# A graph layer and a mixture-of-experts block on one core: rows of x on more transfer engines, edge counts in two groups, four bank pairs in the first layer

## The chip, the cores and the metric

The kernel runs on one core of a Trainium2 chip. The time is device microseconds (us) of one execution. The engines are called as in the profile: PE is TensorE (PEld its weight loads), DVE is VectorE, ACT is ScalarE, POOL is GpSimd, SP is SyncE; SPq and ACTq are their queues of issues.

## The reference

x has 625 rows of 1024 float32; src and dst are 10000 edges, dst sorted.

```python
def layernorm(x): return (x - mean(x)) / sqrt(var(x) + 1e-05)
# graph layer, on xn = layernorm(x), edges (src, dst) and one self edge per row
h = xn @ W.T + b
deg = count of edges (with self) by row = src
out[row] += deg[row]**-0.5 * deg[col]**-0.5 * h[col]
x = x + out
# block, on t = layernorm(x)
h = t @ lin0_w + lin0_b
h = silu(h @ swi1_w1 + swi1_b1) * (h @ swi1_w2 + swi1_b2)
scores = softmax(h @ gate_w.T)                    # 8 experts, the best 4, renormalised
routed = sum over the 4 of weight * (silu(h @ w1) * (h @ w3)) @ w2
shared = (silu(h @ sh_w1) * (h @ sh_w3)) @ sh_w2
h = (routed + shared) @ lin1_w + lin1_b
x = x + silu(h @ swi2_w1 + swi2_b1) * (h @ swi2_w2 + swi2_b2)
```

## The kernel before

**Tiles and units.** The 625 rows are five tiles of TT = 125 rows, in `rows`. Dense layers work on transposed activations [128 features, 8 chunks, 628 tokens] (625 and three of padding, two halves of HT = 314). A *unit* is 128 output features of a layer: one 512 KB block of the weight stream. It comes by SP into one of four `raw` slots. ACT copies it into a rounded high part (`split_hi`, L384) and POOL subtracts that for the low part (`split_lo`, L392). PE multiplies high by high, high by low and low by high (`products`, L1323): 48 matmuls for a unit over two banks, one bank for each half. `half_unit` does one half. A reader on ACT and one on DVE then take the result out of the banks as a high and a low part again. Each engine runs a list written out by hand; semaphores order the engines.

**The start.** SP issues the two index arrays, five transfers for the tiles of x (L344), then the weights. For each tile ACT sums the rows (L530) and the squares (L525). After the last one DVE makes the variance (L834), ACT takes the root (L536), splits the first weight unit and waits for the shift (L839). ACT then normalises tile by tile (L541), PE turns each tile by 8 transposes (`xt_turn`, L1314), ACT and DVE copy the high and the low part (`xt_high` L548, `xt_low` L812).

**Counting edges.** The layer needs the matrix of edge counts, 625 by 625. The edges lie as 80 *slots* of 125. For a slot DVE builds a one-hot of dst (L769) and one of src folded into 314 columns (L770), in which an edge of the upper half weighs 4096 and one of the lower half 1. PE adds 5 matmuls for it into five banks (L1298); `OHR = 4` slots are a *batch* (PE) or *iteration* (DVE), and DVE may be four slots ahead. The slots come in three groups of 32, 32 and 16 (`GROUPS`). A group is opened by 5 matmuls with zeros (L1292) and closed by 5 more (L1304). DVE then decodes each of the five banks into a lower and an upper count (`decode`, L789 to L801); the next group may open when the banks are read (`banks_read`). The first decoding also adds the identity.

**Units of the graph layer.** PE's order is batches 0 to 6, turns 0 and 1, batch 7, closing, turns 2 and 3, the first half of unit 0, turn 4, the second half, unit 1, batches 8 to 11, unit 2, batches 12 to 15, closing, units 3 and 4, the third group (batches 16 to 19), units 5 and 6, the degrees (25 matmuls of one column, L1438), unit 7. Within unit m, PE turns the output of unit m-1 back into rows (`h_turn_first`, L1379) and the last tile of unit m-2 (`h_turn_last`, L1386); these need DVE's low parts `h_low` (L819) and `h_low_last` (L825) of the unit before. ACT and DVE scale the counts by the root of the degrees (L580, L882). Then come ten aggregations and the second normalising (`root`, `ln_high`, `ln_low`, `ln_turn`).

**The first layer, lin0.** Units 0 and 1 are done in halves in banks 0 to 3; units 2 to 7 use banks 0, 1 and 2, 3 in turn, each after DVE's low part of the unit two before (L1520). Ahead of that ACT issues the save of the rows (x1, 2.5 MB, L624) and the load of the gate's weights (L625).

## Time and profile before

| what | us |
|---|---|
| median of 3 runs | 1656.29 |
| lowest and highest | 1655.44, 1656.95 |
| the profiled execution, its own time | 1656.63 |
| its span from first to last instruction | 1655.0 |
| PE busy in the span | 1606.2 |
| DVE, ACT and POOL busy | 491.9, 520.2 and 783.8 |

The time is that of the whole execution; the span runs from the first to the last instruction in the trace. The trace gives start times from the start of the span. A row of a timeline has the start, the time from the first start to the last end of the merged instructions, the engine and line, the operation with its output and inputs, the count, and in brackets the idle time before it with what ended it. A matmul's time holds its way through the array, so pace is read from starts. The granted clock in a window is a share of 2.4 GHz.

### The profile page before, as it was taken

Reading aid. Unit: us, or ns where it says so; the run is one execution under the profiler, and the core shown is the slowest. Engines: PE = TensorE matmul, PEld = TensorE weight load, DVE = VectorE, ACT = ScalarE, POOL = GpSimd, SP = SyncE. Lnnn points to the kernel's source line nnn. Section 1 sums busy time; section 2 is a strip of 40 time slices with the busy share of each in tenths; the row PEclk is TensorE's granted clock in tenths of the full one; section 3 lists DMA queues with packets and bytes.
Section 4 is the critical chain, followed back from the end, with each engine's and each line's share of the span. In section 5 each row is a group of like instructions: output and inputs, shape, how many; then the busy total and the mean of one; then the engine's idle time right before and its main releaser. Section 6 shows DMA issues by size and latency. Waiting matters only on the chain.

```text
span 1655.0 us, 28056 instructions
## 1 busy us (share of the span) xinstructions
PE 1606.2 (97%) x11047; PEld 1588.0 (96%) x11047; DVE 491.9 (30%) x898; ACT 520.2 (31%) x745; POOL 783.8 (47%) x396
## 2 busy tenths in 40 slices
PE   6889989999999999999999999999999899999997
PEld 5789889999999999999999999999999899999997
DVE  5865621111541011414132242424221044111011
ACT  4312123222222234334444434444444222222120
POOL 1211023332352465766767586767677566333330
PEclk8999999999999999999999999999999999999999
DMA  4301032223232254645555464646465566233220
GB/s 128 125 27 39 1 126 77 77 68 126 73 99 77 87 152 130 205 141 183 155 176 170 147 202 140 209 141 209 152 185 156 154 180 181 77 104 111 71 74 34
DMA packets 64355, 205.62 MB, mean 124 GB/s; under 512 B 13228, under 2 KB 14478, under 8 KB 64248
## 3 DMA queue, kind: packets, MB, share of 16 engines
q1 hardware_dynamic: 44718, 157.88, 32.1%
q0 software_dynamic: 14976, 32.81, 6.4%
q10 hardware_dynamic: 4554, 13.32, 2.2%
q8 instruction: 89, 1.46, 0.4%
q14 instruction: 18, 0.15, 0.0%
HBM read 185.01 MB, written 18.95 MB: 123 GB/s over the span
## 4 chain that ended last, share of the span: by engine, by line
PE 91%; DVE 3%; issue 2%; DMA 1%; POOL 1%; ACT 1%; SPq 0%; POOLq 0%; DVEq 0%; ACTq 0%
PE acc L1323 84%; PE acc L1298 2%; DMA rows<-x_dram 1%; PE acc L1603 1%; PE acc L1582 1%; POOL gath L436 1%; POOL w_lo L392 1%; PE acc L1370 0%; DVE yrow L769 0%; DVE gath L801 0%; PE acc L1438 0%; DVE gath L795 0%; DVE gath L793 0%; PE acc L1651 0%; PE acc L1468 0%
## 5 line engine op out<-in xcount | busy, mean ns | idle before, releaser
L392 POOL TENSOR_TENSOR w_lo<-raw,w_hi 128x1024 fp32r<-128x1024 f32 x296 | 713.6, 2419 | 761.6 <-ACT w_hi L384 756.0
L1323 PE MATMUL acc<-act_b,w_hi 128*128 128x314 f32 (+8 forms) x2560 | 518.6, 311 | 0.0
L1323 PE MATMUL acc<-act_x,w_hi 128*128 128x344 f32 (+7 forms) x2048 | 451.7, 309 | 2.3 <-POOL w_lo L392 1.7
L1323 PEld LDWEIGHTS acc<-act_b,w_hi 128*128 128x128 f32 x2560 | 409.9, 189 | 0.0
L1323 PE MATMUL acc<-act_a,w_hi 128*128 128x314 f32 x1792 | 353.3, 314 | 11.3 <-issue 5.4
L1323 PEld LDWEIGHTS acc<-act_x,w_hi 128*128 128x128 f32 x2048 | 342.3, 188 | 3.9 <-issue 3.2
L1323 PE MATMUL acc<-act_b,w_lo 128*128 128x314 f32 (+8 forms) x1280 | 332.1, 308 | 0.0
L384 ACT ACTIVATE w_hi<-raw 128x1024 fp32r<-128x1024 f32 x296 | 310.7, 1050 | 46.2 <-PE acc L1323 34.8
L1323 PE MATMUL acc<-act_x,w_lo 128*128 128x344 f32 (+7 forms) x1024 | 316.3, 309 | 0.0
L1323 PEld LDWEIGHTS acc<-act_a,w_hi 128*128 128x128 f32 x1792 | 288.6, 193 | 12.2 <-issue 5.6
L1323 PEld LDWEIGHTS acc<-act_b,w_lo 128*128 128x128 f32 x1280 | 225.1, 189 | 0.0
L1323 PE MATMUL acc<-act_a,w_lo 128*128 128x314 f32 x896 | 218.7, 311 | 0.0
L1323 PEld LDWEIGHTS acc<-act_x,w_lo 128*128 128x128 f32 x1024 | 192.6, 188 | 0.0
L1323 PEld LDWEIGHTS acc<-act_a,w_lo 128*128 128x128 f32 x896 | 156.2, 192 | 0.0
L1134 DVE TENSOR_TENSOR prod<-acc,silu 128x344 f32<-128x344 f32 x64 | 33.0, 515 | 290.9 <-PE acc L1323 278.3
L1137 DVE TENSOR_TENSOR act_b<-prod,act_b 128x344 fp32r<-128x344 f32 x64 | 99.8, 1559 | 35.7 <-ACT act_b L684 34.6
L684 ACT ACTIVATE act_b<-prod 128x344 fp32r<-128x344 f32 x64 | 31.5, 492 | 187.4 <-DVE prod L1134 173.4
L1126 DVE COPY yrow<-acc 128x256 f32<-128x256 f32 x64 | 27.1, 423 | 165.6 <-PE acc L1603 165.4
L1298 PE MATMUL acc<-yrow 125*125 125x314 bf16 x400 | 62.2, 321 | 13.2 <-DVE yrow L770 13.2
L1298 PEld LDWEIGHTS acc<-yrow 125*125 125x125 bf16 x400 | 58.2, 149 | 17.1 <-DVE yrow L770 15.2
L961 DVE SCALAR_TENSOR_TENSOR prod<-acc,bias,silu 128x628 f32<-128x628 f32 x16 | 13.9, 872 | 192.9 <-PE acc L1323 192.9
L690 ACT ACTIVATE prod<-acc 128x344 f32<-128x344 f32 x64 | 29.3, 457 | 133.4 <-PE acc L1323 133.4
(189 smaller groups left out, 884.1 us busy)
## 6 DMA issues: line engine op xcount, KB each, us to landing
raw<-stream_dram SPq DMA_DIRECT2D x296, 512.0 KB, 3.7
y_dram<-yrow POOLq DMA_DIRECT2D x16, 512.0 KB
rows<-x_dram ACTq DMA_DIRECT2D x2, 2500.0 KB
y_dram<-yrow POOLq DMA_DIRECT2D x8, 352.0 KB
rows<-x_dram SPq DMA_DIRECT2D x5, 500.0 KB
x_dram<-rows ACTq DMA_DIRECT2D x1, 2500.0 KB
h_rows_dram<-rows ACTq DMA_DIRECT2D x1, 2500.0 KB
out_dram<-rows ACTq DMA_DIRECT2D x1, 1250.0 KB
```

The lines of the kernel that those rows point to most:

```text
L384: nc.scalar.activation(w_hi[:, s, :], raw[:, s, :], ACT.Copy).then_inc(hi_split, 1)
L392: nc.gpsimd.tensor_tensor(w_lo[:, s, :], raw[:, s, :], w_hi[:, s, :].bitcast(f32), ALU.subtract).then_inc(lo_split, 1)
L436: pool.indirect_dma_start(out=grow[0:cn, n, :], out_offset=None, in_=h_rows_dram, in_offset=bass.IndirectOffsetOnAxis(ap=now_tok[0:cn, n:n ...
L684: act.activation(g_hi[:, m, :], prod[:, m % 2, 0:CAP], ACT.Copy).then_inc(exp.hi, 1)
L690: act.activation(prod[:, m % 2, 0:CAP], acc[:, m % 4, 0:CAP], ACT.Copy).then_inc(yt_copied, 1)
L1126: dve.tensor_copy(yrow[:, 0:2, m * P:(m + 1) * P], b[:, 0:2 * P].rearrange("p (s d) -> p s d", d=P))
L1134: dve.tensor_tensor(prod[:, m % 2, 0:CAP], acc[:, (2 * m + 1) % 4, 0:CAP], silu[:, 0:CAP], ALU.mult).then_inc(exp.prod, 1)
L1137: dve.tensor_tensor(g_lo[:, m, :], prod[:, m % 2, 0:CAP], g_hi[:, m, :].bitcast(f32), ALU.subtract).then_inc(exp.lo, 1)
L1298: last = pe.matmul(outs[i], oh_dst[0:TT, s, i * TT:(i + 1) * TT], oh_src[0:TT, s, :], start=False, stop=False)
L1323: ins = pe.matmul(o, w, xs_[h], start=(first and w is hi and xs_ is x_hi), stop=(last and w is lo))
L1582: last = pe.transpose(acc[:, TPB + 2 + m % 2, c0:c0 + cn], grow[0:cn, n, m * P:(m + 1) * P], ident[0:cn, 0:cn])
L1603: last = pe.transpose(acc[0:cn, TPB + m % 2, n * P:(n + 1) * P], prod[:, m % 2, c0:c0 + cn], ident[:, :])
```

## The change

The tiles of x come in two transfers each, of 112 and of 13 rows; SP issues tiles 0, 2 and 4, ACT tiles 1 and 3. ACT takes a root of a constant first, and splits the first weight unit ahead of the root of the variance. There are two groups of 40 slots. A group opens with 5 matmuls of one partition that write a negative offset, its last batch carries the closing flag, and the decoding uses 5120 and the offset in place of 4096. Batches and turns alternate from turn 0 on, the low part of h 0 stands before the decoding of the last tile, and the degrees stand before unit 5. ACT saves x1 tile by tile behind each root, and loads the gate's weights before the first root into another buffer. Lin0 uses four pairs of banks.

```diff
@@ -15,7 +15,9 @@
-GROUPS = (32, 32, 16)
+GROUPS = (40, 40)
+BASE = 5120
+BIAS = 2048
@@ -132,7 +134,7 @@
-        gate_raw = gath[:, 0:D]
+        gate_raw = yrow[:, 0, :]
@@ -141,6 +143,7 @@
+        ones16 = scratch16[:, 5416:5416 + 126]
@@ -158,7 +161,7 @@
-        zeros = pw[:, 800:800 + HT // 2].bitcast(bf16)
+        below = pw[:, 800:800 + HT // 2].bitcast(bf16)
...
@@ -336,12 +338,18 @@
+        SPREAD = TT // 16 * 16
+
+        def load_x(eng, i):
+            for r0, r1 in ((0, SPREAD), (SPREAD, TT)):
+                eng.dma_start(rows[r0:r1, i, :], x[i * TT + r0:i * TT + r1, :]).then_inc(x_loaded[i], 16)
+
...
-            for i in range(NT):
-                sp.dma_start(rows[0:TT, i, :], x[i * TT:(i + 1) * TT, :]).then_inc(x_loaded[i], 16)
+            for i in range(0, NT, 2):
+                load_x(sp, i)
@@ -399,7 +407,8 @@
-            pool.memset(zeros[:, :], 0.0).then_inc(const_ready, 1)
+            pool.memset(below[:, :], -float(BASE * BIAS)).then_inc(const_ready, 1)
+            pool.memset(ones16[:, :], 1.0).then_inc(const_ready, 1)
@@ -413,7 +422,7 @@
-            pool.wait_ge(counts_done, len(GROUPS))
+            pool.wait_ge(onehot_used, EC)
@@ -520,21 +529,26 @@
+            for i in range(1, NT, 2):
+                load_x(act, i)
+            act.wait_ge(const_ready, 5)
+            act.activation(rstd[0:TT, 0:1], ones[0:TT, 0:1], ACT.Sqrt)
+
...
-                act.wait_ge(x_loaded[i], 16)
+                act.wait_ge(x_loaded[i], 32)
...
+            split_hi(0, 0)
...
-            split_hi(0, 0)
@@ -572,7 +586,7 @@
-                if m == KC - 1:
+                if m == 5:
@@ -610,26 +624,32 @@
+            def save_x1(i):
+                act.dma_start(x1_dram[i * TT:(i + 1) * TT, :], rows[0:TT, i, :]).then_inc(x1_saved, 16)
+
+            act.dma_start(gate_raw, gate).then_inc(gate_loaded, 16)
...
+            save_x1(0)
...
+            save_x1(1)
...
+            save_x1(2)
...
+            save_x1(3)
...
-            act.wait_ge(gnn_x1, len(AGG))
-            act.dma_start(x1_dram.rearrange("(i p) d -> p i d", p=TT), rows[0:TT, :, :]).then_inc(x1_saved, 16)
-            act.dma_start(gate_raw, gate).then_inc(gate_loaded, 16)
+            save_x1(4)
...
-            def linear_hi(st, o_hi, b):
+            def linear_hi(st, o_hi, b, pairs):
...
-                    act.activation(halves(o_hi[:, m, :]), acc_dense(m % 2), ACT.Identity,
+                    act.activation(halves(o_hi[:, m, :]), acc_dense(m % pairs), ACT.Identity,
@@ -646,7 +666,7 @@
-            linear_hi(lin0, b_hi, B_LIN0)
+            linear_hi(lin0, b_hi, B_LIN0, 4)
@@ -733,7 +753,7 @@
-            linear_hi(lin1, b_hi, B_LIN1)
+            linear_hi(lin1, b_hi, B_LIN1, 2)
@@ -745,7 +765,7 @@
-            act.wait_ge(x1_saved, 16)
+            act.wait_ge(x1_saved, 16 * NT)
@@ -762,16 +782,16 @@
-            link(dve.tensor_scalar(src_v[0:TT, :], src_v[0:TT, :], 4095.0, 1.0, ALU.mult, ALU.add))
-            dve.wait_ge(const_ready, 6 + EXPERTS)
+            link(dve.tensor_scalar(src_v[0:TT, :], src_v[0:TT, :], float(BASE - 1), 1.0, ALU.mult, ALU.add))
+            dve.wait_ge(const_ready, 7 + EXPERTS)
...
-                dve.tensor_scalar(oh_dst[0:TT, s, 0:T], iota[0:TT, 0:T], dst_f[0:TT, j], None, ALU.is_equal)
+                dve.tensor_scalar(oh_dst[0:TT, s, :], iota[0:TT, 0:T + 1], dst_f[0:TT, j], None, ALU.is_equal)
...
-            def iteration(it):
-                for s in range(OHR):
+            def iteration(it, part=range(OHR)):
+                for s in part:
@@ -782,19 +802,19 @@
-                    dve.wait_ge(counts_done, g + 1)
+                    dve.wait_ge(onehot_used, sum(GROUPS[:g + 1]))
...
-                link(dve.tensor_scalar(upper, v, 1.0 / 4096, -0.5 + 2.0 ** -13, ALU.mult, ALU.add))
+                link(dve.tensor_scalar(upper, v, 1.0 / BASE, -0.5 + 2.0 ** -6, ALU.mult, ALU.add))
...
-                    dve.scalar_tensor_tensor(out=low, in0=upper, scalar=-4096.0, in1=v,
+                    dve.scalar_tensor_tensor(out=low, in0=upper, scalar=-float(BASE), in1=v,
...
-                    link(dve.tensor_copy(high, upper))
+                    link(dve.tensor_scalar(high, upper, float(BIAS * len(GROUPS)), None, ALU.add))
...
-                    dve.scalar_tensor_tensor(out=lower_c[0:TT, :], in0=upper, scalar=-4096.0,
+                    dve.scalar_tensor_tensor(out=lower_c[0:TT, :], in0=upper, scalar=-float(BASE),
@@ -833,25 +853,30 @@
-            iteration(5)
+            iteration(5, range(0, 2))
...
+            iteration(5, range(2, OHR))
...
-            for i in range(1, NT):
-                xt_low(i)
-            for i in range(NT):
+            xt_low(1)
+            iteration(8)
+            xt_low(2)
+            iteration(9)
+            xt_low(3)
+            xt_low(4)
+            for i in range(4):
...
-            iteration(8)
...
-            for it in range(9, 13):
+            decode(0, 4)
+            for it in range(10, 16):
...
-            for it in range(13, 16):
+            for it in range(16, 20):
@@ -860,31 +885,28 @@
-            iteration(16)
...
-            for it in range(17, 20):
-                iteration(it)
-            decode(2, 0)
-            decode(2, 1)
-            h_low_last(3)
-            decode(2, 2)
-            h_low(4)
-            decode(2, 3)
-            decode(2, 4)
-            h_low_last(4)
-            h_low(5)
...
-            for i in range(NT):
+
+            def counts_low(i):
...
-                if i == 1:
-                    h_low_last(5)
-            h_low(6)
+
+            counts_low(0)
+            counts_low(1)
+            h_low_last(3)
+            counts_low(2)
+            counts_low(3)
+            counts_low(4)
+            for m in range(4, 7):
+                h_low(m)
+                if m < 6:
+                    h_low_last(m)
@@ -942,10 +964,10 @@
-            def linear_lo(st, o_hi, o_lo, b):
+            def linear_lo(st, o_hi, o_lo, b, pairs):
...
-                    dve.scalar_tensor_tensor(out=halves(o_lo[:, m, :]), in0=acc_dense(m % 2),
+                    dve.scalar_tensor_tensor(out=halves(o_lo[:, m, :]), in0=acc_dense(m % pairs),
@@ -966,14 +988,14 @@
-            linear_lo(lin0, b_hi, b_lo, B_LIN0)
+            linear_lo(lin0, b_hi, b_lo, B_LIN0, 4)
...
-                    dve.wait_ge(x1_saved, 16)
+                    dve.wait_ge(x1_saved, 16 * NT)
...
@@ -1281,7 +1303,7 @@
-            pe.wait_ge(const_ready, 6 + EXPERTS)
+            pe.wait_ge(const_ready, 7 + EXPERTS)
@@ -1289,20 +1311,16 @@
-                    pe.matmul(outs[i], zeros[0:TT, 0:TT], zeros[0:TT, 0:HT], start=True, stop=False)
-
-            def batch(it):
+                    pe.matmul(outs[i], ones16[0:1, 0:TT], below[0:1, 0:HT], start=True, stop=False)
+
+            def batch(it, closes=False):
...
+                    ends = closes and s == OHR - 1
...
-                                         oh_src[0:TT, s, :], start=False, stop=False)
+                                         oh_src[0:TT, s, :], start=False, stop=ends)
...
-
-            def close_counts():
-                for i in range(NT):
-                    last = pe.matmul(outs[i], zeros[0:TT, 0:TT], zeros[0:TT, 0:HT], start=False, stop=True)
-                last.then_inc(counts_done, 1)
@@ -1401,36 +1419,31 @@
                 half_unit(U_GNN, m, a_hi, a_lo, GNN_BANKS[1], 1, turn_first).then_inc(unit_done, 1)
 
             open_counts(0)
-            with pe.Fori(0, 7) as it:
+            with pe.Fori(0, 6) as it:
                 batch(it)
             xt_turn(0)
+            batch(6)
             xt_turn(1)
             batch(7)
-            close_counts()
             xt_turn(2)
-            xt_turn(3)
+            batch(8)
             pe.wait_ge(pads_zero, 2)
             pe.wait_ge(xt_lo, 2 * 3)
             half_unit(U_GNN, 0, a_hi, a_lo, GNN_BANKS[0], 0).then_inc(gnn_half, 1)
+            xt_turn(3)
             xt_turn(4)
+            batch(9, closes=True)
             pe.wait_ge(xt_lo, 2 * NT)
             half_unit(U_GNN, 0, a_hi, a_lo, GNN_BANKS[1], 1).then_inc(unit_done, 1)
             gnn_unit(1)
             open_counts(1)
-            for it in range(8, 12):
+            for it in range(10, 15):
                 batch(it)
             gnn_unit(2)
-            for it in range(12, 16):
-                batch(it)
-            close_counts()
+            for it in range(15, 20):
+                batch(it, closes=it == 19)
             gnn_unit(3)
             gnn_unit(4)
-            open_counts(2)
-            for it in range(16, 20):
-                batch(it)
-            close_counts()
-            gnn_unit(5)
-            gnn_unit(6)
 
             pe.wait_ge(counts_read, NT)
             for r in range(NT):
@@ -1438,6 +1451,8 @@
+            gnn_unit(5)
+            gnn_unit(6)
@@ -1517,8 +1532,9 @@
-                pe.wait_ge(lin0.lo, m - 1)
-                dense(U_LIN0, m, a_hi, a_lo)
+                if m >= 4:
+                    pe.wait_ge(lin0.lo, m - 3)
+                unit(U_LIN0, m, a_hi, a_lo, (2 * (m % 4), 2 * (m % 4) + 1), HT)
```

## Rows read from the trace of the kernel before

**Rows 1.** The page, busy time, share of the span and instructions.

```profile
PE 1606.2 (97%) x11047; PEld 1588.0 (96%) x11047; DVE 491.9 (30%) x898; ACT 520.2 (31%) x745; POOL 783.8 (47%) x396
```

**Rows 2.** Windows: length, busy us (count) of PE, PEld, DVE, ACT, POOL, clock, DMA.

```profile
30.70:38.00 7.30, 7.30 (x40) 6.66 (x41) 6.22 (x16) 3.96 (x5) 2.36 (x1) 0.73 0.22 74
38.00:57.20 19.20, 15.48 (x115) 14.54 (x114) 11.98 (x22) 11.80 (x17) 3.30 (x2) 1.00 0.07 25
57.20:70.40 13.20, 8.56 (x59) 7.97 (x57) 12.75 (x20) 4.35 (x8) 8.79 (x4) 0.94 0.76 214
70.40:103.30 32.90, 32.16 (x217) 31.23 (x218) 22.71 (x65) 2.91 (x6) 2.41 (x1) 0.92 0.21 77
103.40:124.20 20.80, 17.09 (x109) 16.63 (x108) 15.47 (x32) 4.20 (x9) 2.50 (x1) 0.92 0.09 26
124.20:137.00 12.80, 12.07 (x91) 11.78 (x89) 8.97 (x24) 1.62 (x3) 2.41 (x1) 1.00 0.15 42
137.10:169.80 32.70, 31.66 (x211) 31.20 (x210) 18.12 (x32) 10.93 (x21) 4.82 (x2) 0.90 0.12 33
```

**Rows 3.** Chain of waits in order of time: start, us, what.

```profile
228.24 71.82 PE acc L1323 x480
...
1403.62 154.13 PE acc L1323 x1056
```

**Rows 4.** Timeline of PE: start, us, line, operation, count, idle before and releaser.

```profile
5.36 16.18 PE L1298 MATMUL acc<-yrow 125*125 125x314 bf16 x100 [0.71 <-DVE yrow L770]
...
96.06 6.89 PE L1298 MATMUL acc<-yrow 125*125 125x314 bf16 x50 [0.74 <-DVE yrow L770]
...
119.11 0.67 PE L1379 MATMUL acc<-ident,yrow 128*125 128x128 f32 x4 [3.37 <-DVE act_b L825]
...
228.24 0.85 PE L1323 MATMUL acc<-act_a,w_hi 128*128 128x314 f32 x4 [2.73 <-DVE act_b L948]
```

**Rows 5.** Line 344, the issues of x: ns min, median, max.

```profile
L344 SPq DMA_DIRECT2D rows<-x_dram x5: 335/343/3721, 1.7 to 3.3; - x5
```

**Rows 6.** Windows again: x alone, and weight loads.

```profile
9.00:11.00 2.00, 2.00 (x11) 1.76 (x10) 0.71 (x3) 0.97 (x2) 0.00 (x0) 1.00 0.32 133
...
230.00:233.00 3.00, 3.00 (x14) 3.00 (x14) 0.00 (x0) 0.00 (x0) 3.00 (x2) 0.57 0.86 259
```

**Rows 7.** Timeline of ACT and its queue.

```profile
12.72 1.06 ACT L530 ACTIVATE act_b<-rows 125x1024 fp32r<-125x1024 f32 x1 [2.75 <-DMA rows<-x_dram]
...
13.78 1.14 ACT L525 ACTIVATE act_b<-rows,sums 125x1024 fp32r<-125x1024 f32 x1
...
29.85 1.28 ACT L536 ACT_TABLE_LOAD   x1
...
217.06 8.36 ACTq L625 DMA_DIRECT2D gath<-gate_dram  x1
```

**Rows 8.** Timeline of DVE and POOL.

```profile
29.86 0.17 DVE L834 TENSOR_SCALAR mv<-sums 125x5 f32<-125x5 f32 x1 [10.18 <-ACT act_b L525]
...
32.45 2.36 POOL L392 TENSOR_TENSOR w_lo<-raw,w_hi 128x1024 fp32r<-128x1024 f32 x1 [29.42 <-ACT w_hi L384]
32.50 2.49 DVE L769 TENSOR_SCALAR yrow<-yrow,prod 125x625 bf16<-125x625 f16 x1
...
53.90 9.71 POOL L392 TENSOR_TENSOR w_lo<-raw,w_hi 128x1024 fp32r<-128x1024 f32 x4 [19.09 <-ACT w_hi L384]
...
54.46 2.03 DVE L793 CAST gath<-silu 125x314 f32<-125x314 int32 x1
...
64.71 0.32 DVE L793 CAST gath<-silu 125x314 f32<-125x314 int32 x1
...
113.53 2.50 POOL L392 TENSOR_TENSOR w_lo<-raw,w_hi 128x1024 fp32r<-128x1024 f32 x1 [17.98 <-ACT w_hi L384]
...
113.70 2.67 DVE L801 TENSOR_TENSOR gath<-gath,silu 125x314 f32<-125x314 f32 x1
...
118.67 0.29 DVE L825 TENSOR_TENSOR act_b<-acc,act_b 125x128 fp32r<-125x128 f32 x1
```

More of the change, by code:

```diff
@@ L202, in build @@
         onehot_used = sem("onehot_used")
-        counts_done = sem("counts_done")
         counts_read = sem("counts_read")
@@ L1263, in _ @@
                                   ALU.subtract).then_inc(shb_dlo, 1)
-            linear_lo(lin1, b_hi, b_lo, B_LIN1)
+            linear_lo(lin1, b_hi, b_lo, B_LIN1, 2)
             def out_rows(m):
```

## The prediction

> **What bounds the kernel now.** I read the page's busy shares first, then the windows, then the chain of waits, then each engine's timeline. TensorE is busy 97% of the span [rows 1]. From 228 us on the chain is TensorE's matmuls almost throughout; two of its rows [rows 3] show them at full pace, 1056 in 154.13 us or 0.146 each, and 480 of the first layer slower than that. The change touches nothing behind the first layer. So only the stretch before that can give time, and there every microsecond that TensorE idles or runs at the lower clock counts in full.
>
> The windows [rows 2] cut this stretch. TensorE's first 20 slots end at 21.5 [rows 4], the next batch starts at 30.7 and runs at 0.73 of full clock to 38.0 (40 matmuls, 2.0 us lost); 38.0 to 57.2 holds the turns and unit 0, busy 15.48 of 19.20 at full clock; from 57.2 (first matmul of unit 1) to 70.4 (first batch after the first decoding) it is busy 8.56 of 13.20 us; 70.4 to 103.4 holds 32 slots, unit 2 and one closing pass; 103.4 to 124.2 holds units 3 and 4, busy 17.09 of 20.80; 124.2 to 137.0 is the third group; 137.1 to 169.8 units 5, 6, the degrees and unit 7.
>
> Costs of one piece: a slot is 5 matmuls, 50 took 6.89 us with the last one's tail, so 0.67 us a slot [rows 4]. VectorE builds four slots between 116.4 and 118.67 [rows 8], 0.57 each, so a batch runs at TensorE's pace unless VectorE is held. A unit is 48 matmuls at 0.146, 7.0 us, with its turns 7.6.
>
> **First part: the rows of x.** SyncE issues x in five transfers; four issues cost 0.34 us and one 3.72 [rows 5]. While only x moves, the engines are busy 0.32, five of sixteen, at 133 GB/s; weight loads (128 rows) reach 259 GB/s at 0.86 [rows 6], so about 300 GB/s with all engines. Cut into 112 and 13 rows on two queues, 2.56 MB at 300 is 8.5 us, after a start near 2.5 us: x0 and x1 together by 7 us, the last tile by 12.
>
> The page "DMA: Bandwidth & Descriptors" of the Trainium skill says (section "Why a DMA increments its semaphore by 16 and not by 1") that the engine count is the largest number up to 16 that divides the outer dimension: 5 for 125 rows, 16 for 112, 13 for 13. The trace's 0.32 agrees for 125; no row shows a 112-row load. The same page's section "Rules for kernel authors" speaks against the edit: two transfers to disjoint partitions, or two queues, gain nothing. The rival "loads no faster" below is what that would give.
>
> ScalarE then is the limit: sum 1.06 and square 1.14 [rows 7], with the reads of their accumulators 2.28 us a tile, 11.4 for five. From 7.2 us the squares end at 18.6 instead of 29.8. VectorE finishes slot 20 at 19.7 as before (its 10.18 idle ends at 29.86 [rows 8]), TensorE uses it until 21.5. The table load of 1.28 us before the root [rows 7] moves under the wait for x. (If squares need another table than the root, two loads come back; 1.28 in the chain is partly covered, worth 0.7.) The first weight split now stands before the root, so GpSimd's subtraction (2.36 us) starts near 19.8, and a VectorE one-hot that meets it is held until it ends, as 2.49 shows [rows 8]. I charge this: slot 21 is ready at 23.0, not 21.5, and after the split pieces of iteration 5 the shift is ready at 24.1. Normalise 0 ends 25.5, batch 5 ends 26.0, still at full clock.
>
> Then turn, batch, turn, batch. A turn of 8 transposes is 0.95, a batch 2.7. While a batch runs, ScalarE's two copies (1.13) and normalise (1.24) and VectorE's two subtractions (1.27) of the tile before are done, and the four one-hot slots were built one batch ahead, so I charge no wait: turns 0, 1, 2 with batches 6, 7, 8 take 26.0 to 36.9; half-unit 0 to 40.4; turns 3 and 4, with 1.1 us of waits for the bank reads (of the 3.7 that TensorE idles in this window before), to 43.4; batch 9 to 46.1; the second half to 49.6. Before, unit 1 began at 57.2, with 32 slots done. Now it begins at 49.6 with 40 done: **-7.6 us**.
>
> **Second part: two groups and the decodings.** Decoding 0 starts beside the second half-unit, 11.1 us before unit 1 ends; before, 11.3 us. Its steps on SBUF meet GpSimd's four subtractions in a row (9.71 us): the copy takes 2.03 there, 0.32 alone [rows 8]. I step it through: GpSimd ends at 47.5, 50.0, 52.4, 54.8; the first two tiles take until 55.1, tiles 2 and 3 until 58.3, the moved low part of h 0.6, tile 4 frees its bank at 59.9. Unit 1 ends at 57.2, the next subtraction, behind some 1.9 us of ScalarE's copies and split, runs 59.1 to 61.5 and holds the copy again; first slot 62.6. So the gap is 5.4 against the old 5.6 (13.20 less unit 1's 7.6): **-0.2**. The clock falls after it as before (0.92 over the 32.90 us of the next window, some 2.4 us lost), which I leave in.
>
> From there to unit 3: 20+20 slots instead of 16+16, +8 x 0.67 = +5.4, minus one closing pass, 5 matmuls, 0.6: **+4.8**.
>
> Units 3 and 4: TensorE waits 3.37 us for the low part of h [rows 4], since VectorE makes 4 slots of the third group (2.3 us) ahead of it [rows 8]. That goes; what stays is 1.1, too short to lower the clock (3.7 us of shorter waits in 38.0 to 57.2 left 1.00 [rows 2]). With the lower clock after it, 0.92 over this window's 20.80 us, another 1.6 (half of the 3.3 at the lower level): 2.3+1.6 = **-3.9**. Decoding 1's last step meets GpSimd by 0.17 us [rows 8]; if it slips ahead, the 1.1 goes too.
>
> The third group goes, opening, 16 slots, a 0.7 wait and closing, 124.2 to 137.1: **-12.9**. Units 5 to 7: no decoding beside them, most of the 1.04 that TensorE idles in 137.1 to 169.8 [rows 2] goes: **-0.95**. The degrees move two units earlier at the same cost, with the lower clock after them.
>
> **Third part: the first layer and the saves.** At 217.06 ScalarE issues the gate load behind a 2.5 MB save and stays in that issue 8.36 us [rows 7], to 225.4. So unit 0's output isn't read in time: TensorE idles 2.73 before 228.24 [rows 4], of which I take 2.5, and the next 480 matmuls take 71.82 against 70.06 at 0.146 [rows 3], 1.8 more. The gate load now goes out before the roots into an empty queue, each save of 500 KB (3.9 us at 133 GB/s) after its tile, 3.5 us or more apart, under the four issues that pass [rows 5]; and with four bank pairs units 2 and 3 wait for no reader at all. 2.5+1.8 = **-4.3**. Five more issues of 0.3 us on ScalarE lie in its idle time; if each blocked as the gate's did, 8 us each, normalising would be late; nothing in the spacing says so.
>
> **At nothing:** the constants of the decoding, the opening matmul of one partition (same columns), two memsets (0.1 us before a start that waits for the indices), x reloaded 8 us earlier (needed at 150), swi1 (its first banks are read four units before).
>
> **Sum:** -7.6-0.2+4.8-3.9-12.9-0.95-4.3 = -25.05. The profiled execution took 1656.63 us (span 1655.0); 1656.6-25.0 = 1631.6, and the median of the runs is 0.3 lower: **1631.3 us**.
>
> **The rivals.**
> *Loads no faster* (0.08): x still arrives by 26.4. The squares end at 29.8, the table load and split no longer stand behind them, normalise 0 begins at 30.8 instead of 24.3, and the 9 us wait brings the lower clock, 2.0 us. +6.5+2 to +10: 1640 to 1641. Against it: five of sixteen engines' worth of work in 9.0 to 11.0 [rows 6]. It would show as waits of ScalarE for x after the first.
> *The relay* (0.13): if each slot of batches 6 to 9 is built only after the low part of the tile before, the subtractions (1.27) and two slots' one-hots (1.14) are open, 2.4 us four times, +9.6: 1641. For it: TensorE idles 3.7 us among turns and unit 0 now [rows 2]. Against: there most turns had no batch between.
> *No stalls* (0.08): the copy and the last decoding step slip past GpSimd (-1.1), no hold at 19.8 (-1.8), the clock holds after decoding 0 (-2.4): 1626.
> *Slower* (0.03): TensorE's clock. If mixing turns with batches leaves the lower level granted from 26 us on, slots cost 1.3 instead of 0.67 and units double. It decides once 50 us of the 124 up to the aggregation run at the lower level (+25, no gain); if all of them, +62: some 1693. Against: 38.0 to 57.2 with turns and waits ran at 1.00 [rows 2]. The Trainium skill, page "TensorE: Matmul & The Clock Gate", section "Part 4: PE-mode transpose", says that transposes don't count as busy in the same way, which would favour this; these rows don't agree with it at that density.
>
> **How the numbers follow.** My forecast has 0.68, with its own range 1626 to 1637 (the clock after the gap, the hold at 19.8 twice over, the table loads). The range 1624 to 1642 takes in loads, relay and no stalls. About 0.2%, 3.3 us, is what a measurement here can tell. No case but the clock reaches 1653: faster 0.95, same 0.02, slower 0.03.
>
> **What would show it.** ScalarE's square group ending near 19 us and one table load before it; TensorE with no gap over 2 us until the first decoding; a gap near 5 us there and none over 1.5 in units 3 and 4; the degrees' group near 118 us; the first aggregation near 149 instead of 169.8; no idle time in the first layer. The prediction is wrong if the squares end after 22, if the two 20-slot stretches run below 0.67 a slot, or if saves stand long in ScalarE's queue.

## The result, and the profile after

The kernel after took 1631.51 us (median of four runs, 1631.06 to 1632.96) against 1656.62 for the kernel before beside it (four runs, 1655.44 to 1657.34): a ratio of 0.985, 95% interval 0.9838 to 0.9862, 25.1 us less. The profiled execution took 1632.96 us with a span of 1631.3, against 1656.63 and 1655.0: 23.7 less in the trace. The forecast was 1631.3.

The page of after, busy time of each engine: TensorE's fell by 8.7 us against [rows 1], so the other 15.0 of the 23.7 us are idle time that went.

```profile
PE 1597.5 (98%) x11027; PEld 1581.9 (97%) x11027; DVE 474.3 (29%) x878; ACT 519.4 (32%) x745; POOL 788.3 (48%) x397
```

The windows of after, cut near the same events as [rows 2] (columns as there; the events themselves are read from the timelines). A row each: to the first slot, to turn 0, to unit 1, to the first slot of the second group, to unit 3, units 3 and 4, degrees and units 5 to 7.

```profile
0.00:9.20 9.20, 1.56 (x5) 0.95 (x5) 1.59 (x10) 1.50 (x3) 2.20 (x20) 1.00 0.78 202
9.30:28.90 19.60, 18.63 (x120) 17.71 (x121) 17.60 (x53) 14.20 (x24) 2.35 (x1) 1.00 0.63 174
28.90:52.30 23.40, 22.34 (x171) 22.03 (x170) 17.68 (x43) 12.41 (x18) 4.34 (x2) 1.00 0.08 25
52.30:65.80 13.50, 9.07 (x58) 8.20 (x56) 13.05 (x21) 4.37 (x8) 7.73 (x4) 0.86 0.75 204
65.90:102.50 36.60, 35.87 (x254) 35.20 (x254) 27.30 (x80) 2.91 (x6) 2.41 (x1) 0.96 0.19 66
102.60:117.80 15.20, 15.11 (x107) 14.88 (x106) 10.63 (x24) 4.21 (x9) 2.65 (x1) 1.00 0.10 27
117.90:150.50 32.60, 32.60 (x210) 32.60 (x210) 7.24 (x12) 12.56 (x24) 7.11 (x3) 0.84 0.16 51
```

By the first matmul of each in the timelines, unit 1 begins at 52.2 instead of 57.3, unit 3 at 102.4 instead of 103.4 although 8 slots more lie before it, the third group's 12.9 us are gone, and the first aggregation begins at 150.6 instead of 169.8. Units 3 and 4 run at full clock, idle for 0.09 us in all; the stretch with the degrees shows 0.84.

TensorE's timeline: all waits over 0.8 us from the first slot up to the aggregation, and the degrees (25 matmuls in the program, 50 records in the trace):

```profile
9.28 14.64 PE L1321 MATMUL acc<-yrow 125*125 125x314 bf16 x90 [4.49 <-DVE yrow L790]
24.89 4.22 PE L1321 MATMUL acc<-yrow 125*125 125x314 bf16 x30 [0.97 <-DVE yrow L790]
...
45.11 1.14 PE L1332 MATMUL acc<-ident,rows 125*128 125x125 f32 x8 [1.06 <-DVE act_a L832]
...
62.66 1.56 PE L1314 MATMUL acc<-prod,yrow 1*125 1x314 bf16 x5 [2.85 <-DVE gath L811]
65.87 15.02 PE L1321 MATMUL acc<-yrow 125*125 125x314 bf16 x100 [1.65 <-DVE yrow L790]
...
117.86 8.47 PE L1451 MATMUL acc<-ones,gath 125*125 125x1 f32 x50
```

The first slot starts at 9.28 after a wait of 4.49, not at 5.36 [rows 4]; among turns one wait of 1.06 is left; the wait of 3.37 inside unit 4 [rows 4] is gone. ScalarE's timeline (columns as in [rows 7]) shows the single table load, the first tile of x at 10.02, and the last square's end where the weight split starts, 21.20 (before, the squares ended at 29.8):

```profile
3.00 1.28 ACT L535 ACT_TABLE_LOAD   x1 [2.87 <-issue]
...
10.02 1.06 ACT L544 ACTIVATE act_b<-rows 125x1024 fp32r<-125x1024 f32 x1 [5.52 <-DMA rows<-x_dram]
...
21.20 1.04 ACT L392 ACTIVATE w_hi<-raw 128x1024 fp32r<-128x1024 f32 x1
```

VectorE waits for the index arrays to 7.44. Later it is *held*, that is, one step takes as long as a GpSimd subtraction beside it: a one-hot at 22.38 by GpSimd's first subtraction (22.39 for 2.35), steps of the decoding by the four subtractions from 47.96 on (the addition takes 2.37 and 2.36 beside them, the copy 1.49), and a one-hot at 63.20 by the next one (62.97 for 2.39).

```profile
7.44 0.20 DVE L779 CAST prod<-prod 125x80 f32<-125x80 int32 x1 [7.44 <-DMA prod<-src_dram]
```

```profile
22.38 2.46 DVE L790 TENSOR_SCALAR yrow<-yrow,prod 125x314 bf16<-125x314 f16 x1
...
50.57 2.37 DVE L815 TENSOR_TENSOR gath<-gath,ident 125x125 f32<-125x125 f32 x1
...
53.90 1.49 DVE L813 TENSOR_SCALAR gath<-prod 125x314 f32<-125x314 int32 x1
55.42 2.36 DVE L815 TENSOR_TENSOR gath<-gath,ident 125x125 f32<-125x125 f32 x1
...
58.74 0.32 DVE L813 TENSOR_SCALAR gath<-silu 125x314 f32<-125x314 int32 x1
...
63.20 2.35 DVE L789 TENSOR_SCALAR yrow<-yrow,prod 125x626 bf16<-125x626 f16 x1
```

```profile
22.39 2.35 POOL L400 TENSOR_TENSOR w_lo<-raw,w_hi 128x1024 fp32r<-128x1024 f32 x1 [19.21 <-ACT w_hi L392]
47.96 9.68 POOL L400 TENSOR_TENSOR w_lo<-raw,w_hi 128x1024 fp32r<-128x1024 f32 x4 [23.22 <-ACT w_hi L392]
```

In the first layer the chain of waits is one row of 528 matmuls. Before, 48 matmuls were followed by the wait of 2.73 [rows 4] and 480 more that took 71.82 us [rows 3]:

```profile
199.07 77.28 PE acc L1341 x528
```

### The profile page after: what moved, and what is told of

Read it like the earlier page. It is cut to its first block, busy times and chain, and to the rows that moved or that the text cites. A ratio compares the mean times of both kernels' runs of the same rounds, so it can differ in the third digit from the quotient of the medians.

```text
span 1631.3 us, 27998 instructions
## 1 busy us (share of the span) xinstructions
PE 1597.5 (98%) x11027; PEld 1581.9 (97%) x11027; DVE 474.3 (29%) x878; ACT 519.4 (32%) x745; POOL 788.3 (48%) x397
## 4 chain that ended last, share of the span: by engine, by line
PE 94%; DVE 2%; issue 1%; POOL 1%; DMA 0%; ACT 0%; POOLq 0%; DVEq 0%; SPq 0%; ACTq 0%
PE acc L1341 86%; PE acc L1321 3%; PE acc L1619 1%; PE acc L1598 1%; POOL w_lo L400 1%; POOL gath L445 1%; PE acc L1451 1%; PE acc L1388 1%; DVE yrow L790 0%; DVE yrow L789 0%; DMA prod<-src_dram 0%; DVE gath L815 0%; PE acc L1667 0%; PE acc L1332 0%; PE acc L1483 0%
```

## The experiments

Each ran beside the kernel before: e1 to e4 in one set (1655.9 us), e5 to e8 in a second (1656.4), e9 to e12 in a third (1656.6); after itself ran beside 1656.6. A difference between medians of different sets can hold up to 0.7 us that comes from the set; where two figures are given, the second is the difference between the gains over the kernel before of the same set. "After plus" or "before plus" says from which kernel a run is edited.

### The start

**e1**, after plus one wait: ScalarE sends no x until the index arrays have landed.

```diff
+            act.wait_ge(idx_loaded, 32)
             for i in range(1, NT, 2):
                 load_x(act, i)
```

> The changed kernel, but ScalarE issues its tiles of x only after the two index arrays have landed. My theory: in the changed kernel the index arrays (five engines, small packets) share those engines with ScalarE's x from its own queue and land at 7.4 us instead of 3.5, which puts the first batch at 9.3 instead of 5.4. Then here they land by 4, the first batch starts by 5.7, the squares end by 20, the first turn comes 2 to 3 us sooner and the time is 1628.5 to 1630. Rival (the indices are late because the memory is slow to answer with any x in flight): first batch still near 9, time 1631 to 1633.

**e2**, after plus: all ten transfers of x on SyncE's queue, none on ScalarE's.

```diff
-            for i in range(0, NT, 2):
+            for i in range(NT):
                 load_x(sp, i)
...
-            for i in range(1, NT, 2):
-                load_x(act, i)
```

> The changed kernel, but all ten transfers of x on SyncE's queue behind the index arrays. My theory (a second queue overtakes the indices): indices by 4 us, first batch by 5.7, x tiles in order at 260 to 300 GB/s, squares end 19 to 20, time 1628.5 to 1630. Rival (two queues are needed for the rate of x): tiles arrive slower than ScalarE works, squares end after 22, time 1631.5 or more. The other rival, indices late with any x in flight: first batch near 9.

**e3**, after plus: the five loads of 125 rows of the kernel before, everything else as in after.

```diff
-            for i in range(0, NT, 2):
-                load_x(sp, i)
+            for i in range(NT):
+                sp.dma_start(rows[0:TT, i, :], x[i * TT:(i + 1) * TT, :]).then_inc(x_loaded[i], 16)
...
-            for i in range(1, NT, 2):
-                load_x(act, i)
```

> The changed kernel, but x loaded as before: five transfers of 125 rows on SyncE. My theory (the spread is worth what TensorE waited for): first batch at 5.4, squares end near 29, first turn 34 to 35 against 29.0 in the changed kernel, some lower clock behind the wait, time 1637 to 1639. Rival (the arrival of x is hidden by the batches anyway, and the spread costs the late indices): 1628 to 1632.

**e4**, after plus: the first weight split behind the root instead of before it.

```diff
             squares(NT - 1).then_inc(squares_ready, 1)
-            split_hi(0, 0)
             act.wait_ge(var_ready, 1)
             act.activation(rstd[0:TT, :], mv[0:TT, :, 1], ACT.Sqrt).then_inc(root_ready, 1)
+            split_hi(0, 0)
```

> The changed kernel, but the first weight split stands behind the root of the variance again. My theory: GpSimd's subtraction then starts after VectorE has written the shift, so the one-hot held from 22.4 to 24.8 goes, the root comes at 22.8 instead of 25.5, and the hold meets a later one-hot with slots in store; time 1629.5 to 1631. Rival (the hold is only moved, TensorE loses the same 1 us a little later): 1631.5, and a gap of 1 us between 26 and 30.

| | median, us (range) | ratio to before [95%] | first slot | squares end | turn 0 |
|---|---|---|---|---|---|
| after | 1631.51 (1631.06 to 1632.96) | 0.985 [0.9838, 0.9862] | 9.28 | 21.2 | 28.9 |
| e1 | 1633.56 (1632.69 to 1634.36) | 0.9867 [0.9851, 0.9884] | 5.28 | 23.6 | 30.1 |
| e2 | 1627.12 (1626.45 to 1627.99) | 0.9826 [0.9809, 0.9842] | 5.38 | 17.9 | 24.2 |
| e3 | 1638.96 (1638.38 to 1640.51) | 0.9897 [0.9881, 0.9914] | 5.18 | 29.5 | 36.1 |
| e4 | 1632.05 (1630.97 to 1632.29) | 0.9857 [0.9841, 0.9874] | 9.05 | 21.2 | 27.9 |

ScalarE's timeline of e1: its own tile, x1, asked for from 3.44 on, when SyncE had already issued most of its tiles, comes at 13.82.

```profile
3.44 1.99 ACTq L345 DMA_DIRECT2D rows<-x_dram  x4
...
13.82 1.06 ACT L545 ACTIVATE act_b<-rows 125x1024 fp32r<-125x1024 f32 x1 [5.83 <-DMA rows<-x_dram]
```

The same in e2: x0 at 6.22 and x1 at 8.10, and no wait for x after that.

```profile
6.22 1.06 ACT L542 ACTIVATE act_b<-rows 125x1024 fp32r<-125x1024 f32 x1 [3.72 <-DMA rows<-x_dram]
...
8.10 1.06 ACT L542 ACTIVATE act_b<-rows 125x1024 fp32r<-125x1024 f32 x1 [0.73 <-DMA rows<-x_dram]
```

The index arrays land at 3.3 to 3.5 when nothing of x goes out beside them from ScalarE (e1, e2, e3), at 7.4 when it does. With e1 the wait only moved to x1: the first slot came early, as I expected, but the time, 1633.56, is later than my 1628.5 to 1630 and than the rival's 1631 to 1633. In e2 both come in order, and the kernel is 4.4 (3.7) us faster than after, 1.4 us better than I expected. The second queue is a loss here, not a help.

The trace's rows for the queues show it. q10 is ScalarE's and q1 SyncE's (e2, where only SyncE issues, has q1 alone). A row gives packets, MB and share of 16 engines, first of after up to 4 us, then up to 10 us:

```profile
q10 hardware_dynamic: 127, 0.45, 35.6%
q1 hardware_dynamic: 107, 0.08, 10.4%
```

```profile
q1 hardware_dynamic: 551, 1.10, 45.3%
q10 hardware_dynamic: 290, 0.99, 35.3%
```

By 4 us ScalarE's queue had moved 0.45 MB and SyncE's, with the index arrays at its head, 0.08. By 10 us nearly four tiles' worth had come, two of them ScalarE's, and only then was x0 complete. In TensorE's timeline of e3 the squares set the pace again:

```profile
30.42 2.88 PE L1319 MATMUL acc<-yrow 125*125 125x314 bf16 x10 [10.11 <-DVE yrow L788]
...
36.08 1.02 PE L1330 MATMUL acc<-ident,rows 125*128 125x125 f32 x8
```

e2 and e3 differ in the cut of the tiles alone: the spread over more transfer engines is worth 11.8 us. (After is 7.4 (8.2) us ahead of e3, with the spread and the second queue together; my 1637 to 1639 for e3 held.) e4 moved the hold of VectorE (2.53 us at 23.68) and turn 0 came 1 us earlier; its profiled span is 2.0 us shorter, but the medians don't tell the two apart: 1632.05 is what the rival said (1631.5), not my 1629.5 to 1631.

### The first layer and the saves

**e5**: before plus the saves by tile and the gate load ahead of the roots. **e6**: before plus the four bank pairs. **e10**: before plus both.

```diff
# e5
-        gate_raw = gath[:, 0:D]
+        gate_raw = yrow[:, 0, :]
...
+            act.dma_start(gate_raw, gate).then_inc(gate_loaded, 16)
             root(0)
+            save_x1(0)
...
-            act.wait_ge(gnn_x1, len(AGG))
-            act.dma_start(x1_dram.rearrange("(i p) d -> p i d", p=TT), rows[0:TT, :, :]).then_inc(x1_saved, 16)
-            act.dma_start(gate_raw, gate).then_inc(gate_loaded, 16)
+            save_x1(4)
# e6, whose readers go by the same four pairs
-                pe.wait_ge(lin0.lo, m - 1)
-                dense(U_LIN0, m, a_hi, a_lo)
+                if m >= 4:
+                    pe.wait_ge(lin0.lo, m - 3)
+                unit(U_LIN0, m, a_hi, a_lo, (2 * (m % 4), 2 * (m % 4) + 1), HT)
```

> The kernel before with one part of the change alone: the gate's weights go into another buffer ahead of the roots, x1 is saved tile by tile; lin0 keeps two bank pairs. My theory (ScalarE stood in the issue of the gate load and read unit 0 late): the wait of 2.7 us before unit 2 of lin0 and the lower clock behind it go, -4.3 us, 1651.6. Rival (two pairs need a wait there anyway, since both halves of units 0 and 1 end together): the wait stays at 1.5 us or more, 1654 or later.

> The kernel before with four bank pairs in lin0 alone; ScalarE still issues the 2.5 MB save and the gate load ahead of it. My theory: ScalarE still stands in that issue for 8 us, but units 2 and 3 need no reader, so TensorE doesn't wait: also -4.3 us, 1651.6; the two edits are each enough and don't add. Rival (ScalarE's late splits of the weights for unit 3 hold TensorE): -2 us or less, 1654.

> The kernel before with both edits of the third part, the saves and the four pairs. The two alone gave 1652.8 and 1651.5 against 1656.4. If each is enough: 1651 to 1652.5, no more than the better of them. Rival (they add): 1648 to 1649.

e5: 1652.78 (1650.56 to 1653.47), ratio 0.9975 [0.9966, 0.9985]. e6: 1651.54 (1650.51 to 1651.85), 0.9969 [0.9957, 0.9982]. e10: 1651.76 (1650.73 to 1652.98), 0.9972 [0.9962, 0.9981]. ScalarE's queue in e6 still stands 8.37 us in the gate's issue, and yet the chain shows the layer without a wait:

```profile
217.54 8.37 ACTq L625 DMA_DIRECT2D gath<-gate_dram  x1
```

```profile
218.75 77.30 PE acc L1323 x528
```

e5 shows the same row with two bank pairs (528 in 77.27 from 219.72), and e10 too (77.27 from 218.34). Before, the same 528 took from 218.27 to 300.06, 81.8 us. So each edit alone takes the whole 4.5 us in the layer, and they don't add. The time of e6 (1651.6 expected) and of e10 (1651 to 1652.5) came as expected; e5 is 1.2 us above the 1651.6 I expected, though its layer is as fast as e6's.

### The gap before the second group, and the alternation

**e7**, after plus unit 2 ahead of the second group: TensorE has matmuls while VectorE decodes.

```diff
             gnn_unit(1)
+            gnn_unit(2)
             open_counts(1)
             for it in range(10, 15):
                 batch(it)
-            gnn_unit(2)
+            gnn_unit(3)
             for it in range(15, 20):
                 batch(it, closes=it == 19)
-            gnn_unit(3)
             gnn_unit(4)
+            gnn_unit(5)
...
# VectorE
             decode(0, 4)
-            for it in range(10, 16):
-                iteration(it)
+            iteration(10)
             h_low_last(0)
             h_low(1)
+            for it in range(11, 16):
+                iteration(it)
...
```

> The changed kernel with one unit more between the two groups: units 1 and 2, group 2's batches 10 to 14, unit 3, batches 15 to 19, units 4 and 5, degrees, units 6 and 7. My theory (the decoding of group 1, slowed by GpSimd, is what TensorE waits for before group 2): the 5.4 us of idle time around the opening and the 1.7 us of lower clock behind it go, 1624 to 1626. Rival (the decoding is merely slower beside another unit's subtraction, or the low part of h 0 and 1 then comes late): 1629 to 1632, with waits inside units 2 and 3.

**e8**: e2 and e7 together.

> All of x on SyncE's queue and unit 2 before the second group, together. If the two gains lie in different places, they add: 1627.1 less 6.5, 1619 to 1622. If the same low clock is counted in both, 1623 to 1625.

**e9**, after plus turns and batches in the order of the kernel before.

```diff
-            with pe.Fori(0, 6) as it:
+            with pe.Fori(0, 7) as it:
                 batch(it)
             xt_turn(0)
-            batch(6)
             xt_turn(1)
             batch(7)
+            batch(8)
+            batch(9, closes=True)
             xt_turn(2)
-            batch(8)
+            xt_turn(3)
...
             half_unit(U_GNN, 0, a_hi, a_lo, GNN_BANKS[0], 0).then_inc(gnn_half, 1)
-            xt_turn(3)
             xt_turn(4)
-            batch(9, closes=True)
```

> The changed kernel with the turns and batches in the order of before: turns 0 and 1, batches 7 to 9, turns 2 and 3, first half of unit 0, turn 4, second half. My theory: the alternation hides ScalarE's and VectorE's copies behind batches; without it TensorE idles some 3 us among the turns as it did before, against 1.1, and the decoding starts beside turn 2 instead of behind all of them only in part; +1.5 to +3, 1633 to 1634.5. Rival (batches cover nothing, the order is worth nothing): 1631 to 1632.

**e11**: e8, with the last low part of h ahead of tile 4 of decoding 0.

```diff
             h_low(0)
-            decode(0, 4)
-            iteration(10)
             h_low_last(0)
+            decode(0, 4)
+            iteration(10)
             h_low(1)
```

> All of x on SyncE's queue, unit 2 ahead of the second group, and the last low part of h 0 built before the decoding of tile 4. In the run with unit 2 first, TensorE waited 3.6 us inside unit 2 for that low part, which stood behind four one-hot slots and a held decoding step. My theory: that wait goes, and no other takes its place before batch 10: 1621 to 1623. Rival (the next item in VectorE's list is as late, so the wait moves to the opening of the group): 1624 to 1626.

**e12**, after plus: GpSimd lets decoding 0 read its banks before its further subtractions.

```diff
-            for o in range(3):
+            for o in range(2):
                 split_lo(0, o)
+            pool.wait_ge(banks_read, NT)
+            split_lo(0, 2)
```

> The changed kernel, but GpSimd makes the low weights of units 2 and on only after the five banks of group 1 are read. My theory (a VectorE step on SBUF that meets a subtraction stands until it ends, about one step per 2.4 us): the decoding of tiles 1 to 3 loses its holds and takes 1.6 us a tile, and the four subtractions then meet the one-hots instead, so the second group starts later than in the changed kernel (67 or more against 65.9) and its first slots come slowly: 1633 to 1637. Rival (VectorE is slowed by something else in that stretch): decoding as slow as before, 1631 to 1632.

| | median, us (range) | ratio to before [95%] |
|---|---|---|
| e7 | 1629.24 (1628.81 to 1630.26) | 0.9837 [0.9821, 0.9854] |
| e8 | 1625.52 (1623.16 to 1626.52) | 0.981 [0.9794, 0.9826] |
| e9 | 1631.15 (1630.73 to 1633.65) | 0.9853 [0.9836, 0.9869] |
| e11 | 1621.60 (1620.49 to 1622.45) | 0.9789 [0.9772, 0.9805] |
| e12 | 1634.02 (1633.61 to 1635.73) | 0.9865 [0.9848, 0.9881] |

TensorE's timeline of e7: the gap before the group is gone, a wait of 3.55 has come in its place, inside unit 2, for the low part of h. That is the rival that I had named (1629 to 1632, waits inside the units), not my 1624 to 1626; the gain over after is 2.3 (2.1) us.

```profile
67.08 1.19 PE L1400 MATMUL acc<-ident,yrow 128*125 128x128 f32 x4 [3.55 <-DVE act_b L845]
```

In e8 it is 3.59, and the two edits give 6.0 (5.8) us against 4.4 and 2.3 for e2 and e7. Its four runs lie 3.4 us apart, so whether they add in full can't be told; 1625.52 is above both of my ranges (1619 to 1622, 1623 to 1625), which counted on a larger gain from e7. VectorE makes that part behind tile 4 of the decoding, one step of which GpSimd holds (61.69 for 2.34 in e7, 59.15 for 2.35 in e8), and four one-hots. e11 takes it out of that queue, and the wait is gone, as expected (1621 to 1623); the longest wait left in its timeline from the decoding to the aggregation is this one:

```profile
67.87 10.91 PE L1322 MATMUL acc<-yrow 125*125 125x314 bf16 x80 [0.78 <-DVE yrow L788]
```

e12 shows who holds VectorE. Without subtractions beside it, a tile is decoded in 1.6 us. Then the four in a row meet the end of the decoding and the one-hots, and each of the four steps beside them takes one subtraction's time:

```profile
59.43 9.38 POOL L400 TENSOR_TENSOR w_lo<-raw,w_hi 128x1024 fp32r<-128x1024 f32 x4 [9.32 <-DVE gath L813]
```

```profile
59.62 2.32 DVE L817 TENSOR_TENSOR gath<-gath,ident 125x125 f32<-125x125 f32 x1
61.98 2.34 DVE L791 TENSOR_SCALAR yrow<-yrow,prod 125x626 bf16<-125x626 f16 x1
...
66.54 2.46 DVE L791 TENSOR_SCALAR yrow<-yrow,prod 125x626 bf16<-125x626 f16 x1
```

The group opens without a wait there, but TensorE waits 6.30 us before its first slot, against 2.85 and 1.65 around the opening in after, and the kernel is 2.5 us slower, as expected (1633 to 1637; the first slot at 66.67, where I had said 67 or more). Moved onto the slots, the subtractions cost more than beside the decoding; e11 shows that matmuls can cover them.

e9 missed what I expected (1633 to 1634.5). Its turns and batches do wait (0.55, 0.50, 1.13 and 1.56, and 3.75 before the second group), and its first layer begins 3.1 us later, at 202.18 against 199.07. But it ends no later. The windows of 1200 to 1300 us, after first and then e9, show where the profiled execution gets it back, in a place that no edit touches:

```profile
1200.00:1300.00 100.00, 94.25 (x665) 93.77 (x664) 13.81 (x32) 34.50 (x48) 63.45 (x31) 0.97 0.52 156
```

```profile
1200.00:1300.00 100.00, 96.78 (x699) 96.05 (x698) 13.81 (x32) 36.24 (x50) 67.72 (x33) 1.00 0.56 167
```

TensorE idles 5.75 us in the one and 3.22 in the other, and the clock is 0.97 against 1.00, worth 3 us of 100: 5.5 together, of which the spans show 4.9. The chain in after has one piece of idle time there, in e9 two shorter ones with matmuls between:

```profile
1270.70 4.19 issue
```

```profile
1272.35 0.85 issue
1273.20 2.12 PE acc L1339 x13
1275.33 2.15 issue
```

So the alternation is worth 3.1 us up to the first layer, and e9's profiled execution got more than that back later. Of the ten traces of after and its variants only e9's shows 1.00 there; the other nine have one idle piece of 4.0 to 4.2 us and 0.97 or 0.98. Why it fell so is open, and so is whether it did in e9's other three executions; one of them took 1633.65 us, which is what I had expected.

## Why the prediction was right, and where two terms were off

The median was right to 0.2 us, and part of that is luck: the sum for the profiled execution, 1631.6, missed by 1.4 (23.7 us less instead of 25.05), but the profiled execution happened to be the slowest of the four, and the median lies 1.45 below it. Two terms were clearly mis-sized, in opposite directions: the start by 2.5 and units 3 and 4 by 1.5. Most of the gain is work that is no longer done (the third group, 12.9, against 3.6 for the longer two); no run has the two groups alone, so those terms rest on the trace of after. By the first matmul of the same events in both traces:

| step | forecast | measured |
|---|---|---|
| start, to unit 1 | -7.6 | -5.1 |
| unit 1 and the gap | -0.2 | +0.5 |
| to unit 3 | +4.8 | +3.6 |
| units 3 and 4 | -3.9 | -5.4 |
| third group | -12.9 | -12.9 |
| degrees, units 5 to 7 | -0.95 | 0.0 |
| first layer and saves | -4.3 | -4.5 |
| sum (before rounding) | -25.05 | -23.7 |

**The start (-7.6, came -5.1).** The step that failed is "x0 and x1 together by 7 us", and with it "From 7.2 us the squares end at 18.6". I charged nothing for what two queues do to each other and to the index arrays at the head of SyncE's. The first tile was ready at 10.02, and the index arrays, which I left where they were, came at 7.44, so that TensorE waited 4.49 us before its first slot, where I had named no gap over 2 us until the decoding as a sign. The squares took 11.2 us, as in the sum, but ended at 21.2 instead of 18.6; turn 0 began at 28.9 instead of 26.0, and from there to unit 1 it was 23.3 us, forecast 23.6. e2 shows the cause: with one queue the squares end at 17.9 and turn 0 begins at 24.2. Held VectorE and the single table load came as charged.

The rate wasn't at fault. In e2 from 4 to 6 us only x is under way (the first weights are issued at 5.90), and the transfer engines are busy 1.02 at 297 GB/s, against my 300. In after, with x and weights in flight from 4 to 10 us, they are busy 1.04 at 260. First e2, then after:

```profile
4.00:6.00 2.00, 1.42 (x7) 0.81 (x6) 1.86 (x10) 0.00 (x0) 0.00 (x0) 1.00 1.02 297
```

```profile
4.00:10.00 6.00, 1.51 (x7) 0.91 (x6) 2.39 (x12) 0.49 (x2) 0.00 (x0) 1.00 1.04 260
```

That all are busy in e2, where [rows 6] had 0.32 for x, agrees with the rule of the Trainium skill on the engine count, page "DMA: Bandwidth & Descriptors", section "Why a DMA increments its semaphore by 16 and not by 1". The rule against the edit (same page, "Rules for kernel authors") has to be split. It says that transfers on several queues don't help the bandwidth; the runs agree and go further, since here the second queue cost 4.4 (3.7) us. It says that two transfers to disjoint partition halves gain nothing, and gives as its reason that both halves use all 16 engines. A tile of 125 rows ran on five, so the reason doesn't hold for it, and 112 and 13 rows gained 11.8 us on one queue (e2 against e3); my text had left the reason out. The rival "loads no faster" was priced well by e3, 1638.96 for 1640 to 1641.

**The gap (-0.2, came +0.5).** Its mechanism, VectorE's SBUF steps held one at a time by GpSimd's subtractions, is what the timelines and e12 show. ScalarE's split for the next unit waited 1.22 us for its weights (to 61.74), which I had not in the sum. GpSimd's subtraction then met the first one-hot, at 63.20, and not a step of the decoding as forecast.

**To unit 3 (+4.8, came +3.6).** The clock was 0.96 of full over 36.6 us instead of the 0.92 over 32.9 that I left in, which is 1.2 us less lost.

**Units 3 and 4 (-3.9, came -5.4).** The 1.1 us that I kept went too, and an earlier wait of 0.34: decoding 1's last addition started at 112.28, ahead of the subtraction at 112.35, and took 0.48. That was named as possible. The margin is small, but no chance of one execution: in all ten traces of after and its variants the addition starts 0.07 to 0.09 us ahead and takes 0.48.

**Degrees and units 5 to 7 (-0.95, came 0).** The waits went. But the 50 one-column matmuls took 8.47 us, and the clock was at the lower level longer: 0.76 in 117.9 to 122, 0.50 in 122 to 130 and 0.96 in 130 to 134 here; before, 0.84 in 152 to 160 and 0.78 in 160 to 169.8. By length times what is missing to 1.00, that is 5.1 us against 3.4, an estimate that gives back more than the 1.0 of the waits; the trace shows 0.0 for both.

```profile
117.90:122.00 4.10, 4.10 (x32) 4.10 (x31) 0.00 (x0) 1.62 (x3) 2.15 (x1) 0.76 0.06 24
122.00:126.00 4.00, 4.00 (x21) 4.00 (x21) 0.00 (x0) 0.00 (x0) 0.19 (x1) 0.50 0.43 131
126.00:130.00 4.00, 4.00 (x17) 4.00 (x18) 1.85 (x3) 1.77 (x4) 0.00 (x0) 0.50 0.00 0
```

```profile
152.00:160.00 8.00, 8.00 (x61) 8.00 (x60) 0.65 (x1) 1.62 (x3) 2.35 (x1) 0.84 0.19 52
160.00:169.80 9.80, 9.80 (x57) 9.80 (x57) 5.27 (x8) 5.12 (x9) 0.00 (x0) 0.78 0.10 39
```

**First layer (-4.3, came -4.5).** Right in size: 2.5 for the wait and 1.8 for the slower 480 matmuls behind it. The 1.8 is the lower clock that followed the wait ([rows 6] has 0.57 in 230 to 233, and the clock is 1.00 again from 234 on); with the wait gone, it goes too, and either edit alone takes both. The five saves were issued in 0.26 to 0.28 us each, as assumed.

**The rivals.** The relay didn't come: one wait of 1.06 among turns. Nor did the clock: 28.9 to 52.3, turns among batches, ran at 1.00, which doesn't bear out what the Trainium skill says of transposes, page "TensorE: Matmul & The Clock Gate", section "Part 4: PE-mode transpose", at the density of 8 transposes to 20 matmuls. "No stalls" came in part: the last step of the decoding slipped ahead, but the one-hot at 22.38 was held, and the clock fell after decoding 0 (0.86 in 52.3 to 65.8).

## What to carry to other kernels

Before small transfers on which the first work hangs, don't open a second queue with large ones: order on one queue was worth 4.4 (3.7) us more than two. Where another engine's work holds VectorE a step at a time, what helped here was not to move that work but to put a unit of matmuls over it, and then to look at what stands next in VectorE's list: covering alone gave 2.3 (2.1) us here, covering with the one step moved ahead 3.9 (4.1) more (e11 against e8), and e11 is the fastest of all, 1621.60 us.

## What was not expected of the hardware

- A small transfer is late when large ones of another queue are under way: the index arrays landed at 7.4 instead of 3.3 to 3.5 us. So is a large one asked for late: x1, asked for from 3.44 on beside SyncE's, at 13.82.
- Behind one idle piece of 4.0 to 4.2 us near 1270 us the clock was lower in all nine traces that have it (0.97 or 0.98 over 1200 to 1300; in after 0.89 over 1275 to 1300); in e9, with two pieces of 0.85 and 2.15 and 13 matmuls between, it stayed at 1.00. What happens 1000 us behind an edit can hide what the edit is worth.
- The 50 records of one-column matmuls took 8.47 us in after, 6.97 in before and 6.49 in e12. The clock goes with it: in their first 4 us it was 0.77, 0.98 and 1.00, and in the 4 us after that 0.50, 0.50 and 0.54. Why it fell earlier in one than in the other is open.
